# Local attention: dividing probabilities before their transposes instead of scaling the outputs after

## The chip, the cores and the metric

The kernel runs on one core of one Trainium2 chip. The metric is the device time of one execution in microseconds (us). Engines are named as in the profile: PE (TensorE), DVE (VectorE), ACT (ScalarE), POOL (GpSimd), SP (the queue that starts most DMAs).

## What is computed

The reference takes x of 4 batches x 1024 tokens x 256 features. A causal attention with 16 heads comes first; after it come two layers (DEPTH = 2), each with a local attention of 8 heads of 64 features and a feed-forward part. The change lies in the local attention, which in the reference is, cut to what matters:

```python
q = l2norm(q) * qs
k = l2norm(k) * ksc
q, k = rotary_xpos(q, k)
bq = q.reshape(b, h, w, WINDOW, d) * QK_SCALE          # WINDOW = 128
bk, bv = look_around(bk), look_around(bv)              # own window and the one before: 256 keys
sim = jnp.einsum('bhwid,bhwjd->bhwij', bq, bk)
sim = jnp.where(mask, -jnp.finfo(sim.dtype).max, sim)
attn = jax.nn.softmax(sim, axis=-1)
out = jnp.einsum('bhwij,bhwjd->bhwid', attn, bv)
x = x + o @ wo
```

## The kernel before

The program has four stages one after another: `prepare`, `causal_attention` and `project_causal` (up to some 745 us), then `layers`, which holds all that the change touches. `layers` works through eight batches (`it` 0 to 7: two layers of four batches), each as `attention(it)` and then `feed_forward(it)`. A batch has 8 windows of 128 tokens. A window has four units (`PAIRS` = 4) of two heads each, so `attention` runs over 32 units `u`, with w = u // 4 and p = u % 4. Each engine has its own stream, written out by hand as a loop over `u`; its instructions run in that order and wait on counting semaphores for the others.

What one step `u` issues, engine by engine:

- **PE**: `scores` for the units u and u+1 when u is even (L1348, into two PSUM banks), `turn_probs(u-2)` (L1419: four 128x128 transposes of the probabilities), `turn` of the next window's rotated q and k in the steps with p = 0 and 1 (L1328), `project` of the window three ahead in p = 1, 2, 3 (L1302, one third each), and `values` for two units when u is even (L1444). In p = 2 it also has `spread_sums` (L1428), which transposes the widened inverses of the window before. Step 21 and 22 have `project_out` (L1364), 24 and 29 the transposes around the layer norm.
- **ACT**: `copy_probs(u-2)` (L1616), `exponentials(u)` (L1600: two activations with the row sum as second result), the copies of turned q and k (L1592), the high half of x (L1577), `square` (L1563, p = 2), `copy_v` (L1585, p = 3), `widen_sums` (L1625, p = 1) and `copy_output` (L1632, p = 2).
- **DVE**: `mask_scores(u)` (L1865: adds the mask, writes p_sb and the row minimum, for two heads), `unit_vectors(w+2)` in p = 0 (L1842), `times_sin(w+2)` in p = 1 (L1856, four instructions), `low_x` in p = 2 (L1830), `sums(w+3)` in p = 3 (L1836), `invert_sums` (L1917, p = 1) and `scale_output` (L1923, p = 3).
- **POOL**: `rotate`: two multiplications with the cosines (L1758), then, once the four of `times_sin` are done, one addition (L1763); and `norms`: a clamp (L1748) and a power (L1750), which turn the sums of squares into the inverse norms that `unit_vectors` waits for.

The softmax sums are used late before the change: the probabilities go unscaled through transposes and the product with the values, and the output of a window is multiplied afterwards by inverses that have been inverted (DVE), widened (ACT), transposed (PE) and applied (DVE).

## Time and profile before

| what | value |
|---|---|
| median of 3 runs | 2187.49 us (2186.98 to 2192.35) |
| the profiled execution | 2186.37 us, its span 2184.6 us |
| mean granted TensorE clock | 0.968 of full |
| busy: PE, DVE, ACT, POOL | 90%, 66%, 58%, 35% of the span |

The page gives each engine's busy time as a share of the whole span, then the span in 40 slices, the chain of work that ended last, and the costliest groups of instructions. `layers` fills the slices from the fifteenth on. Its attention parts take some 92 us of each batch and its feed-forward parts some 80 us. A line of the timeline is one or several merged instructions of an engine: start, length, engine, line, what is written from what, and in brackets how long the engine sat idle before it and who released it.

### The profile page before, as it was taken

The numbers are of one execution on the slowest core, as the hardware profiler recorded it, in microseconds if no ns is written. First come the engines' busy times: TensorE is split into PE (matmuls) and PEld (weight loads), VectorE is DVE, ScalarE is ACT, GpSimd is POOL, SyncE is SP. The second block draws the span as 40 slices with busy tenths as digits, with TensorE's granted clock in tenths as the row PEclk, the third lists the DMA queues.
The fourth block names the chain that finished last, engine by engine and source line by source line (L and its number), as shares of the span: only waits on it lengthen the run. The fifth ranks groups of instructions, "written<-read, shape, count | busy, mean of one in ns | idle before, by whom it ended". The sixth has DMA issues, their size and how long they took to land.

```text
span 2184.6 us, 36290 instructions
## 1 busy us (share of the span) xinstructions
PE 1969.9 (90%) x12096; PEld 1249.0 (57%) x12096; DVE 1436.6 (66%) x3920; ACT 1264.2 (58%) x3012; POOL 759.6 (35%) x639
## 2 busy tenths in 40 slices
PE   7978999999897459999998999999999999999998
PEld 4522333333224247776676676676677677677666
DVE  7788888888853447557567557656656755755754
ACT  4526666666673227547646746745754764754763
POOL 1033121122322356136236326435515605613620
PEclk9969999999998779999999999999999999999999
DMA  6666533544404610000000000023001000000000
GB/s 181 166 116 139 69 54 50 69 64 87 113 9 134 187 70 13 20 20 2 20 11 11 2 30 11 1 80 111 1 20 39 1 20 20 21 20 20 20 1 30
DMA packets 105271, 112.21 MB, mean 51 GB/s; under 512 B 49708, under 2 KB 84096, under 8 KB 104064
## 3 DMA queue, kind: packets, MB, share of 16 engines
q1 hardware_dynamic: 104512, 100.97, 20.4%
q0 software_dynamic: 576, 8.91, 1.0%
q8 instruction: 100, 1.64, 0.3%
q14 instruction: 83, 0.68, 0.1%
HBM read 67.12 MB, written 42.47 MB: 50 GB/s over the span
## 4 chain that ended last, share of the span: by engine, by line
PE 40%; DVE 11%; ACT 8%; issue 5%; POOL 2%; DMA 0%; SPq 0%; DVEq 0%; POOLq 0%; ACTq 0%
PE qkv_ps L1302 6%; PE s_ps L1406 5%; DVE rot_s L1856 4%; PE s_ps L1348 4%; PE pt_ps L1419 3%; PE o_ps L1487 3%; PE pt_ps L1487 3%; PE qkv_ps L1364 3%; PE o_ps L1444 3%; ACT p_sb L1600 3%; DVE p_sb L1865 3%; PE pt_ps L1406 2%; PE o_ps L1406 2%; PE s_ps L1364 2%; POOL inv_norm L1750 2%
## 5 line engine op out<-in xcount | busy, mean ns | idle before, releaser
L679 ACT ACTIVATE probs<-st_ps 128x512 f32<-128x512 f32 (+3 forms) x768 | 330.0, 494 | 165.6 <-PE st_ps L584 165.1
L1302 PE MATMUL qkv_ps<-w_qkv,x_parts 128*128 128x512 f32 x1152 | 309.1, 412 | 33.6 <-DVE x_parts L1830 24.5
L1600 ACT ACTIVATE p_sb<-p_sb,negmax 128x256 f32<-128x256 f32 (+1 forms) x512 | 249.4, 490 | 65.0 <-DVE negmax L1865 64.8
L569 PE MATMUL s_ps<-k_stack,q_stack 96*128 96x512 bf16 (+3 forms) x768 | 242.6, 347 | 36.6 <-DVE piece_negmax L724 25.6
L724 DVE CUSTOM_DVE_ANT_0 seen<-s_ps,causal 128x128 f32<-128x128 f32 (+3 forms) x512 | 233.8, 484 | 42.1 <-PE s_ps L569 42.0
L1302 PEld LDWEIGHTS qkv_ps<-w_qkv,x_parts 128*128 128x128 f32 x1152 | 212.2, 194 | 81.4 <-issue 39.6
L584 PE MATMUL st_ps<-q_stack,k_stack 98*128 98x512 bf16 (+3 forms) x768 | 241.3, 335 | 12.3 <-ACT probs L679 10.1
L1865 DVE CUSTOM_DVE_ANT_0 p_sb<-s_ps,band 128x256 f32<-128x256 f32 (+1 forms) x512 | 185.5, 401 | 88.7 <-PE s_ps L1348 83.8
L806 POOL TENSOR_SCALAR_AFFINE_SELECT probs<-probs 128x512 f32<-128x512 f32 x128 | 81.6, 637 | 414.5 <-ACT probs L679 414.5
L1758 POOL TENSOR_TENSOR rot_c<-qn,turn_by 128x512 f32<-128x512 f32 x128 | 178.6, 1415 | 129.5 <-PE turn_ps L1328 103.6
L1616 ACT COPY p_t<-pt_ps 128x512 f32<-128x512 f32 (+1 forms) x256 | 143.2, 559 | 125.6 <-PE pt_ps L1419 124.4
L1856 DVE TENSOR_TENSOR rot_s<-qn,turn_by 128x256 f32<-128x256 f32 x256 | 202.9, 851 | 0.3
L727 DVE TENSOR_REDUCE piece_negmax<-s_ps 128x1 f32<-128x512 f32 x256 | 176.0, 687 | 29.4 <-PE s_ps L569 29.1
L1750 POOL TENSOR_TENSOR inv_norm<-sum_sq,neg_half 128x16 f32<-128x16 f32 x64 | 187.6, 2932 | 5.3
L1763 POOL TENSOR_TENSOR rot_c<-rot_c,rot_s 128x1024 f32<-128x1024 f32 x64 | 158.7, 2480 | 60.5 <-DVE rot_s L1856 60.5
L1348 PE MATMUL s_ps<-k_t,q_t 64*128 64x256 f32 (+1 forms) x1152 | 139.5, 364 | 32.0 <-DVE negmax L1865 30.6
L601 PE MATMUL o_ps<-probs,v_all 128*32 128x512 f32 (+3 forms) x1536 | 166.1, 505 | 1.2 <-POOL probs L806 0.7
L1419 PE MATMUL pt_ps<-ident,p_sb 128*128 128x128 f32 x960 | 160.8, 287 | 6.1 <-ACT p_t L1616 6.1
L584 PEld LDWEIGHTS st_ps<-q_stack,k_stack 98*128 98x128 bf16 x768 | 72.1, 98 | 159.4 <-ACT probs L679 124.6
L569 PEld LDWEIGHTS s_ps<-k_stack,q_stack 96*128 96x128 bf16 x768 | 75.7, 99 | 149.5 <-DVE piece_negmax L724 71.4
L1836 DVE TENSOR_REDUCE sum_sq<-squares 128x16 f32<-128x1024 f32 x64 | 77.9, 1217 | 111.4 <-ACT squares L1563 111.4
L1348 PEld LDWEIGHTS s_ps<-k_t,q_t 64*128 64x128 f32 x1152 | 93.0, 187 | 79.8 <-issue 68.4
(145 smaller groups left out, 3452.7 us busy)
## 6 DMA issues: line engine op xcount, KB each, us to landing
qk_scratch<-parts SPq DMA_DIRECT2D x64, 192.0 KB, 2.8
q_stack<-qk_scratch SPq DMA_DIRECT2D x96, 128.0 KB, 6.6
k_stack<-qk_scratch SPq DMA_DIRECT2D x96, 128.0 KB, 7.0
w_ffn<-ffn_weights POOLq DMA_DIRECT2D x4, 2176.0 KB, 11.3
x_in<-xt_scratch SPq DMA_DIRECT2D x16, 512.0 KB, 4.1
ffn_weights<-w_high SPq DMA_DIRECT2D x2, 2176.0 KB, 7.6
ffn_weights<-w_raw SPq DMA_DIRECT2D x2, 2176.0 KB, 13.3
att_scratch<-att SPq DMA_DIRECT2D x32, 128.0 KB, 2.0
```

Source lines behind the costliest of these rows:

```text
L569: pe.matmul(s_ps[i % 3][:, 0:kw], q_stack[0:STK, slot, h, qt * P:(qt + 1) * P], k_stack[0:STK, slot, h, k0:k0 + kw], start=True, stop=True ...
L584: pe.matmul(st_ps[i % 3][:, q0:CH], k_stack[0:STK + SHIFT, slot, h, kt * P:(kt + 1) * P], q_stack[0:STK + SHIFT, slot, h, c * CH + q0:(c + ...
L679: act.activation(probs[:, n % 3, h, q0:CH], st_ps[i % 3][:, q0:CH], ACT.Exp).then_inc(exp_done.sem, 1)
L724: dve.tensor_tensor_reduce(seen[:, i % 3, 0:kw], s_ps[i % 3][:, 0:kw], causal[:, CH - kw:CH], -1.0, BIG, ALU.add, ALU.min, result).then_in ...
L1302: mm = pe.matmul(qkv_ps[:, part * CH:(part + 1) * CH], x_parts[:, w % XR, xp, k, :], w_qkv[:, wp, k, part * INNER:(part + 1) * INNER], sta ...
L1348: mm = pe.matmul(s_ps[side][:, to:to + (t1 - t0) * P], q_t[r, w % 2, p, :], k_t[r, p, t0 % KR * P:(t0 % KR + t1 - t0) * P], start=True, st ...
L1406: mm = pe.matmul(up_pair(c, j)[bank][0:rows, :], w_up(w, k, tile)[:, 0:rows], hn_t[:, h, k, :], start=n == 0, stop=n == len(steps) - 1)
L1419: mm = pe.transpose(pt_ps[:, (h * 2 + kt) * P:(h * 2 + kt + 1) * P], p_sb[:, u % 4, h, kt * P:(kt + 1) * P], ident[:, :])
L1600: act.activation(p_sb[:, u % 4, h, k0:PW], p_sb[:, u % 4, h, k0:PW], ACT.Exp, scale=-1.0, bias=negmax[:, u % 4, h:h + 1], accum_out=total[ ...
L1750: pool.tensor_tensor(inv_norm[:, :], sum_sq[:, 1, :], neg_half[:, 0:2 * H2], ALU.pow)\
L1856: dve.tensor_tensor(dst[:, :, o], src[:, :, i], turn_by[:, w, 2 * j + 1, o].unsqueeze(1) .to_broadcast([P, H2, half]), ALU.mult).then_inc( ...
L1865: dve.tensor_tensor_reduce(p_sb[:, u % 4, h, k0:PW], s_ps[u % 2][:, h * PW + k0:(h + 1) * PW], band[:, k0:PW], 1.0, BIG, ALU.add, ALU.min, ...
```

## The change

Every unit's probabilities are now multiplied by the inverses of their sums in place, by DVE, before PE transposes them. `divide(u)` waits for both exponentials of unit u, takes the reciprocal of two sums per partition, waits for its own result, and multiplies p_sb (128 x 512 elements, 128 x 256 in a batch's first window) with the two inverses, broadcast over 256 columns each. It stands at the head of DVE's step u+1. `turn_probs(u)` waits for it instead of for the exponentials. `invert_sums`, `widen_sums`, `spread_sums` and `scale_output` are gone, with their semaphores and the tile inv_wide; the projection of the outputs waits for ACT's copy.

```diff
-        total = sb("total", [P, 2, PAIRS, 2])
-        inv_total = sb("inv_total", [P, 2, PAIRS, 2])
-        inv_wide = sb("inv_wide", [P, H2, HD2])
+        total = sb("total", [P, 4, 2])
+        inv_total = sb("inv_total", [P, 4, 2])
...
-                if w >= 3 and j == 0:
-                    pe.wait_ge(o_scaled.sem, o_scaled.of(it, w - 3))
...
-                pe.wait_ge(o_scaled.sem, o_scaled.of(it, t1 // P - 1))
+                pe.wait_ge(o_copied.sem, o_copied.of(it, t1 // P - 1))
...
                 def turn_probs(u):
-                    pe.wait_ge(exp_done.sem, exp_done.of(it, 2 * u + 1))
+                    pe.wait_ge(divided.sem, divided.of(it, u))
...
-                def spread_sums(w):
-                    pe.wait_ge(widened.sem, widened.of(it, w))
-                    pe.wait_ge(turn_copied.sem, turn_copied.of(it, 2 * min(w + 2, NT - 1) + 1))
-                    for p in range(PAIRS):
-                        mm = pe.transpose(turn_ps[:, p * P:(p + 1) * P], inv_wide[:, 2 * p:2 * p + 2, :], ident[:, :])
-                    mm.then_inc(spread.sem, 1)
...
-                if u % PAIRS == 0:
-                    act.wait_ge(inv_sum.sem, inv_sum.of(it, w - 2))
...
-                                   accum_out=total[:, w % 2, place(u, h)[0], place(u, h)[1]:place(u, h)[1] + 1]).then_inc(exp_done.sem, 1)
+                                   accum_out=total[:, u % 4, h:h + 1]).then_inc(exp_done.sem, 1)
...
-                def widen_sums(w):
-                    act.wait_ge(inv_sum.sem, inv_sum.of(it, w))
...
-                def invert_sums(w):
-                    dve.wait_ge(exp_done.sem, exp_done.of(it, 2 * (w + 1) * PAIRS - 1))
...
-                def scale_output(w):
-                    dve.wait_ge(spread.sem, spread.of(it, w))
-                    dve.wait_ge(o_copied.sem, o_copied.of(it, w))
...
+                def divide(u):
+                    k0 = 0 if u // PAIRS else WIN
+                    dve.wait_ge(exp_done.sem, exp_done.of(it, 2 * u + 1))
+                    dve.reciprocal(inv_total[:, u % 4], total[:, u % 4]).then_inc(inv_sum.sem, 1)
+                    dve.wait_ge(inv_sum.sem, inv_sum.of(it, u))
+                    probs = p_sb[:, u % 4, :, k0:PW]
+                    dve.tensor_tensor(probs, probs, inv_total[:, u % 4, :].unsqueeze(2).to_broadcast([P, 2, PW - k0]),
+                                      ALU.mult).then_inc(divided.sem, 1)
 
                 for u in range(UNITS + 4):
                     w, p = u // PAIRS, u % PAIRS
+                    if 1 <= u <= UNITS:
+                        divide(u - 1)
                     if p == 2 and w + AHEAD + 1 < NT:
                         low_x(it, w + AHEAD + 1)
```

Where DVE's order changes first: the rows from the q and k of `unit_vectors` to the `sums` of a middle window (L1842 unit_vectors, L1865 mask_scores, L1856 times_sin, L1830 low_x, L1836 sums). Before:

```order
L1842 TENSOR_TENSOR qn<-qkv_ps,inv_norm 128x1024 [waits sin_ready,cos_ready,inv_ready]
L1865 ISA p_sb,negmax<-s_ps,band 128x256 [waits s_ready2,pt_ready]
...
L1917 RECIPROCAL inv_total<-total 128x8 [waits widened,exp_done2]
L1856 TENSOR_TENSOR rot_s<-qn,turn_by 128x8x32 [waits rot_ready,qn_ready]
L1856 TENSOR_TENSOR rot_s<-qn,turn_by 128x8x32 x3
L1830 TENSOR_TENSOR x_parts<-x_in,x_parts 128x256 [waits x_high]
L1865 ISA p_sb,negmax<-s_ps,band 128x256 [waits s_ready2,pt_ready]
...
L1836 TENSOR_REDUCE sum_sq<-squares 128x16 [waits clamped,squared]
```

After (the same steps; L1815 is unit_vectors, L1838 mask_scores, L1829 times_sin, L1803 low_x, L1809 sums, L1889 and L1892 are divide):

```order
L1815 TENSOR_TENSOR qn<-qkv_ps,inv_norm 128x1024 [waits sin_ready,cos_ready,inv_ready]
L1889 RECIPROCAL inv_total<-total 128x2 [waits exp_done2]
L1892 TENSOR_TENSOR p_sb<-p_sb,inv_total 128x512 [waits inv_sum]
...
L1829 TENSOR_TENSOR rot_s<-qn,turn_by 128x8x32 x3
L1889 RECIPROCAL inv_total<-total 128x2 [waits exp_done2]
L1892 TENSOR_TENSOR p_sb<-p_sb,inv_total 128x512 [waits inv_sum]
L1803 TENSOR_TENSOR x_parts<-x_in,x_parts 128x256 [waits x_high]
...
L1892 TENSOR_TENSOR p_sb<-p_sb,inv_total 128x512 [waits inv_sum]
L1809 TENSOR_REDUCE sum_sq<-squares 128x16 [waits clamped,squared]
```

A reciprocal and a multiplication now stand between `unit_vectors` and the next mask, between `times_sin` and `low_x`, and ahead of `sums`; the reciprocal of eight sums is gone.

On PE, step p = 2 of a middle window before:

```order
L1348 MATMUL s_ps<-k_t,q_t 128x256 [waits s_masked,turn_copied]
L1348 MATMUL s_ps<-k_t,q_t 128x256 x3
L1419 MATMUL pt_ps<-ident,p_sb 128x128 [waits pt_copied,exp_done2]
L1419 MATMUL pt_ps<-ident,p_sb 128x128 x3
L1428 MATMUL turn_ps<-ident,inv_wide 128x128 [waits turn_copied,widened]
L1428 MATMUL turn_ps<-ident,inv_wide 128x128 x3
L1302 MATMUL qkv_ps<-w_qkv,x_parts 128x512 [waits qn_ready]
```

and after:

```order
L1343 MATMUL s_ps<-k_t,q_t 128x256 [waits s_masked,turn_copied]
L1343 MATMUL s_ps<-k_t,q_t 128x256 x3
L1414 MATMUL pt_ps<-ident,p_sb 128x128 [waits pt_copied,divided]
L1414 MATMUL pt_ps<-ident,p_sb 128x128 x3
L1299 MATMUL qkv_ps<-w_qkv,x_parts 128x512 [waits qn_ready]
```

The four transposes of inv_wide are gone, and the transposes of the probabilities wait for DVE's `divided` instead of ACT's exponentials.

## Rows read from the trace of the kernel before

**Rows 1.** Page, part 1: busy time, share of the span and instructions of each engine.
```profile
PE 1969.9 (90%) x12096; PEld 1249.0 (57%) x12096; DVE 1436.6 (66%) x3920; ACT 1264.2 (58%) x3012; POOL 759.6 (35%) x639
```

**Rows 2.** Busy time by stretch (from:to in us, length, busy us of each engine, PE clock).
```profile
1174.00:1200.00 26.00, 24.18 (x189) 18.38 (x188) 19.69 (x52) 20.06 (x54) 16.88 (x10) 1.00 0.00 1
```

**Rows 3.** Chain that ended last, in order of time (start, length, engine, tile, line).
```profile
1183.12 0.34 DVE x_parts L1830
...
1184.92 0.57 ACT squares L1563
```

**Rows 4.** Timeline of one window (start, length, engine, line, operation; in brackets idle time before).
```profile
1177.62 1.22 DVE L1842 TENSOR_TENSOR qn<-qkv_ps,inv_norm 128x1024 f32<-128x1024 f32 x1 [0.49 <-POOL inv_norm L1750]
...
1178.76 0.41 DVE L1865 CUSTOM_DVE_ANT_0 p_sb<-s_ps,band 128x256 f32<-128x256 f32 x1
...
1179.56 3.56 DVE L1856 TENSOR_TENSOR rot_s<-qn,turn_by 128x256 f32<-128x256 f32 x4
...
1179.68 2.82 POOL L1758 TENSOR_TENSOR rot_c<-qn,turn_by 128x512 f32<-128x512 f32 x2 [2.09 <-PE turn_ps L1328]
...
1183.04 0.41 DVE L1830 TENSOR_TENSOR x_parts<-x_in,x_parts 128x256 fp32r<-128x256 f32 x1
1183.26 2.44 POOL L1763 TENSOR_TENSOR rot_c<-rot_c,rot_s 128x1024 f32<-128x1024 f32 x1 [0.76 <-DVE rot_s L1856]
1183.38 0.41 DVE L1865 CUSTOM_DVE_ANT_0 p_sb<-s_ps,band 128x256 f32<-128x256 f32 x1
...
1185.86 1.22 DVE L1836 TENSOR_REDUCE sum_sq<-squares 128x16 f32<-128x1024 f32 x1 [1.72 <-ACT squares L1563]
...
1187.00 0.41 DVE L1865 CUSTOM_DVE_ANT_0 p_sb<-s_ps,band 128x256 f32<-128x256 f32 x1
...
1187.91 1.13 PE L1348 MATMUL s_ps<-k_t,q_t 64*128 64x256 f32 x8 [0.51 <-DVE negmax L1865]
...
1188.36 0.19 ACT L1600 ACTIVATION_READ_ACCUMULATOR p_sb<-p_sb,negmax 128x1 f32 x1
...
1190.15 0.51 ACT L1600 ACTIVATE p_sb<-p_sb,negmax 128x256 f32<-128x256 f32 x1
...
1190.58 1.23 DVE L1842 TENSOR_TENSOR qn<-qkv_ps,inv_norm 128x1024 f32<-128x1024 f32 x1 [0.49 <-POOL inv_norm L1750]
```

**Rows 5.** One tile's and one line's instructions: ns least/median/most.
```profile
L1917 DVE RECIPROCAL inv_total<-total x64: 196/198/204, 822.9 to 2114.5; 128x8 f32<-128x8 f32 x64
L1428 PE MATMUL turn_ps<-ident,inv_wide x256: 272/273/328, 825.6 to 2118.6; 128*128 128x128 f32 x128
```

**Rows 6.** Timeline, a feed-forward stretch: DVE work beside POOL work.
```profile
1121.69 1.42 DVE L1856 TENSOR_TENSOR rot_s<-qn,turn_by 128x256 f32<-128x256 f32 x4
...
1123.04 0.68 DVE L1964 TENSOR_TENSOR hidden<-gate,hidden 128x512 fp32r<-128x512 f32 x1
...
1123.27 2.72 POOL L1763 TENSOR_TENSOR rot_c<-rot_c,rot_s 128x1024 f32<-128x1024 f32 x1 [1.44 <-DVE rot_s L1856]
...
1124.48 1.79 DVE L1830 TENSOR_TENSOR x_parts<-x_in,x_parts 128x256 fp32r<-128x256 f32 x1
...
1133.83 2.93 POOL L1750 TENSOR_TENSOR inv_norm<-sum_sq,neg_half 128x16 f32<-128x16 f32 x1
...
1135.06 0.41 DVE L1830 TENSOR_TENSOR x_parts<-x_in,x_parts 128x256 fp32r<-128x256 f32 x1
```

**Rows 7.** Timeline, DVE in the sixth window.
```profile
1222.89 0.43 DVE L1865 CUSTOM_DVE_ANT_0 p_sb<-s_ps,band 128x256 f32<-128x256 f32 x1 [1.23 <-PE s_ps L1348]
```

**Rows 8.** Timeline, PE from the seventh window to the last unit.
```profile
1228.60 1.13 PE L1348 MATMUL s_ps<-k_t,q_t 64*128 64x256 f32 x8
...
1248.69 0.66 PE L1419 MATMUL pt_ps<-ident,p_sb 128*128 128x128 f32 x4
```

**Rows 9.** Timeline and busy time where the granted clock fell in the second batch.
```profile
989.95 1.44 PE L1348 MATMUL s_ps<-k_t,q_t 64*128 64x256 f32 x8 [2.03 <-DVE negmax L1865]
...
990.50:994.00 3.50, 3.50 (x21) 2.20 (x18) 1.90 (x5) 2.30 (x8) 2.35 (x1) 0.52 0.03 7
```

More of the change, by code:

```diff
@@ L1144, in layers @@
         exp_done = count("exp_done2", 2 * UNITS)
-        inv_sum = count("inv_sum", NT, 2)
-        widened = count("widened", NT)
-        spread = count("spread", NT)
-        o_scaled = count("o_scaled", NT)
+        inv_sum = count("inv_sum", UNITS)
+        divided = count("divided", UNITS)
         pt_ready = count("pt_ready", UNITS, 4)
@@ L1462, in attention @@
                         final_tiles(it - 1, 1, 1, turn_ps)
-                    if u >= PAIRS + 2 and (u - 2) % PAIRS == 0:
-                        spread_sums((u - 2) // PAIRS - 1)
                     if p >= 1 and w + AHEAD < NT:
@@ L1618, in copy_probs @@
                        .then_inc(pt_copied.sem, 1)
-                def widen_sums(w):
-                    act.wait_ge(inv_sum.sem, inv_sum.of(it, w))
-                    if w:
-                        act.wait_ge(spread.sem, spread.of(it, w - 1))
-                    act.copy(inv_wide[:, :, :], inv_total[:, w % 2].rearrange("p a s -> p (a s)").unsqueeze(2)
-                             .to_broadcast([P, H2, HD2])).then_inc(widened.sem, 1)
                 def copy_output(w):
@@ L1648, in attention @@
                         copy_v(it, w + AHEAD)
-                    if u >= PAIRS + 1 and (u - 1) % PAIRS == 0:
-                        widen_sums((u - 1) // PAIRS - 1)
                     if u >= PAIRS + 2 and (u - 2) % PAIRS == 0:
@@ L1814, in _ @@
         def _(dve):
-            for c in (qn_ready, sin_ready, s_masked, inv_sum, mid_ready, hn_t_split, hidden_ready, hidden_split, out_ready):
+            for c in (qn_ready, sin_ready, s_masked, mid_ready, hn_t_split, hidden_ready, hidden_split, out_ready):
                 dve.sem_inc(c.sem, c.credit)
@@ L1912, in attention @@
             def attention(it):
-                def invert_sums(w):
-                    dve.wait_ge(exp_done.sem, exp_done.of(it, 2 * (w + 1) * PAIRS - 1))
-                    if w >= 2:
-                        dve.wait_ge(widened.sem, widened.of(it, w - 2))
-                    dve.reciprocal(inv_total[:, w % 2], total[:, w % 2]).then_inc(inv_sum.sem, 1)
-                def scale_output(w):
-                    dve.wait_ge(spread.sem, spread.of(it, w))
-                    dve.wait_ge(o_copied.sem, o_copied.of(it, w))
-                    window = o_t[:, :, w % WPC * P:(w % WPC + 1) * P]
-                    dve.tensor_tensor(window, turn_ps[:, :].rearrange("p (h t) -> p h t", h=PAIRS), window, ALU.mult)\
-                       .then_inc(o_scaled.sem, 1)
+                def divide(u):
[6 more added lines that the diff above has]
+                                      ALU.mult).then_inc(divided.sem, 1)
                 for u in range(UNITS + 4):
                     w, p = u // PAIRS, u % PAIRS
+                    if 1 <= u <= UNITS:
+                        divide(u - 1)
                     if p == 2 and w + AHEAD + 1 < NT:
@@ L1933, in attention @@
                         mask_scores(it, u)
-                    if u >= PAIRS + 1 and (u - 1) % PAIRS == 0:
-                        invert_sums((u - 1) // PAIRS - 1)
-                    if u >= PAIRS + 3 and (u - 3) % PAIRS == 0:
-                        scale_output((u - 3) // PAIRS - 1)
                     if it > B and u in (1, 3):
```

## The prediction

> **What bounds the kernel now.** I read the busy shares first: PE 90%, DVE 66% [rows 1]. That looks like a kernel bound by PE, and the change takes work from PE. So I looked at a stretch of two middle windows: in 26 us PE is busy 24.18, DVE 19.69, ACT 20.06 [rows 2]. PE is nearly full there, but the chain that ended last does not stay on it. In each window it runs through DVE's `times_sin`, `low_x`, `mask_scores`, ACT's exponentials and squares, DVE's `sums` and POOL's power (two of its links are shown) [rows 3]. The timeline of one window gives the loop in numbers [rows 4]. I call the start of `unit_vectors` Q (1177.62). `mask_scores` of p = 1 starts at Q+1.14, `times_sin` at Q+1.94 and issues its last at about Q+5.1, `low_x` starts at Q+5.42, the mask of p = 2 at Q+5.76, and `sums` at Q+8.24, when the exponentials and the squares behind that mask are done (2.48 after it). The next `unit_vectors` follows 4.72 after `sums` (1185.86 to 1190.58), because POOL must clamp and raise to a power first. 5.76 + 2.48 + 4.72 = 12.96, the window's period. PE has no term in this loop. So what counts is how late the mask of p = 2 comes after Q, and whether `unit_vectors` stays tied to `sums`.
>
> `times_sin` holds the key. Its four instructions take 1.42 us when POOL leaves them alone (the first line of that stretch) [rows 6], and 3.56 here, with POOL's two cosine multiplications (2.82 us) beside them [rows 4]. In the feed-forward part a `low_x` that takes 0.41 us elsewhere took 1.79: it started 1.21 us into a POOL addition and ended 0.28 us after it [rows 6]. So a DVE instruction with two SBUF inputs stands still until the POOL multiplication or addition has ended. The masks and `unit_vectors`, which read PSUM, do not: the mask of p = 2 takes 0.41 inside the addition [rows 4].
>
> **What the change adds and removes.** A `divide` is a reciprocal (0.20 us for eight sums [rows 5]; I take the same for two), the wait for its own result (no row has one; between nothing and 0.2, I take 0.14, nearest to the 0.145 between `times_sin`'s end and POOL's start [rows 4]) and a multiplication of 128x512 with two SBUF inputs, for which the nearest row is 0.68 [rows 6], some 0.61 from issue to issue. That is 0.95 us, between 0.80 and 1.05, four per window; 0.8 us of old DVE work goes.
>
> In the loop, from Q:
> - The divide of p = 0 stands behind `unit_vectors`: Q+1.14 to Q+2.09. The mask of p = 1 then ends at Q+2.78. POOL's cosine multiplications still start at Q+2.06, so `times_sin` begins inside the first of them; it loses less than it started late, since in both kernels it waits for both of POOL's. It catches up to a last start of Q+5.42, 0.34 later than now.
> - The divide of p = 1 stands right behind it, where `low_x` stood. Its reciprocal starts at Q+5.76 and its multiplication would at Q+6.1. POOL's addition starts 0.145 after the last sine product, at Q+5.98, and takes 2.44. The multiplication has two SBUF inputs, so it waits to Q+8.41 and ends its issue at Q+9.0. `low_x` follows, and the mask of p = 2 starts at Q+9.34 instead of Q+5.76: **3.6 us later**.
> - The divide of p = 2 waits for exponentials that end 1.55 after their mask (1187.00 to 1188.55 [rows 4]), and 1.55 + 0.95 = 2.50, as long as the squares take (2.48). It costs nothing, but if ACT's squares were earlier it would cost all of its 0.95.
> - The divide of p = 3 ends 1.14 + 1.55 + 0.95 = 3.64 after the start of `sums`; the mask behind it ends at 4.33, before 4.72. POOL's power hides it, with 0.4 us to spare.
>
> Period: 9.34 + 2.48 + 4.72 = 16.5 against 12.96. Five windows of a batch have `sums` and `times_sin` (the first with narrower units, the fifth without `low_x`; I take 3.6 for each): 18.0 us. In the sixth the mask of p = 2 waits for PE anyway, at Q+6.7 (1222.89, idle 1.23 until the scores [rows 7]), and two products with w_out keep PE full after it; the late mask is hidden there, and I take 0, with up to 1.5 if that cover is thin.
>
> The windows seven and eight have no rotation. There a pair of units now is one round: scores to the first exponential 2.24 (1187.91 to 1190.15), both exponentials 1.10, a divide 0.95, the second mask to the next scores 0.91 (1187.00 to 1187.91) [rows 4]: 5.2. Three rounds are 15.6. From the last scores to the last transposes it is 2.24 + 1.10 + 0.95, then mask to exponential 0.45, exponentials 1.10, divide 0.95 and 0.1: 6.9. Together 22.5, against 20.09 now (1228.60 to 1248.69 [rows 8]); less 0.44 for the last transposes of inv_wide: plus 2.0, between 0.5 and 3.5.
>
> On PE four transposes per window go. They are 0.27 us each and overlap, at most 0.60 for four by their pipelined starts and ends [rows 5]; in five windows they lie outside the loop and bring nothing. ACT loses a wide copy per window, also outside it. No DMA moves.
>
> PE will stand idle in the longer windows, in one piece of some 2.7 us ahead of the scores of p = 0. Now it idles 2.03 us at one such place in a batch's first window, and in the second batch the granted clock fell to 0.52 of full (so to the 1.2 GHz level) for the 3.5 us behind it; the scores took 1.44 instead of 1.13 [rows 9, 4]. Half of 40 windows with such a fall, some 1 us of PE's work later each, half of it reaching the loop, is 10 us; between 0 and 40.
>
> **Sum:** 8 batches x (18.0 + 0 + 2.0) = 160, and 10 for the clock: 170 us on the profiled execution's 2186.4 is 2356.4. The median of the runs shown lies 1.1 higher, so I say **2357 us**, 7.8% slower. (Within 0.3%, 6.6 us, is what a measurement of this kernel can't tell from no change.)
>
> The Trainium skill, page "SBUF — State Buffer", section "Who interferes with whom", says that a DVE instruction with two SBUF inputs contends with a GpSimd one that reads SBUF, and that whoever issues first keeps the shared port for its whole instruction. For the cosine products and the addition the trace agrees (1.79 against 0.41 us). By the letter of that rule POOL's power would block the divide of p = 3 too; that is rival 3.
>
> **Rivals.**
> 1. The multiplication goes first. It misses POOL's addition by only 0.12 us (Q+6.1 against Q+5.98). If it wins, `low_x` is the one that waits (that happened in [rows 6]), and in four windows nothing changes; only the fifth, without `low_x`, gains 2.3. 8 x 2.3 = 18 less: 2339. For it: the small margin. Against it: the wait for its own result. Chance 0.17.
> 2. The multiplication isn't held and neither is `low_x`, so only DVE's own work counts: 0.34 + 0.95 = 1.3 per window. 8 x (5 x 1.3 + 2.0) = 68: 2255. Against it: the 1.79 us. For it: no row shows a multiplication right behind `times_sin`, and a hold depends on who is first. Chance 0.08.
> 3. POOL's power holds it as well. The power starts 1.75 after `sums` and ends at 4.68; the multiplication of p = 3 would start at 3.0, wait to 4.68, and `unit_vectors` would come at 6.0 instead of 4.72: 1.3 in 40 windows, 50 us more, 2407. Against it: a `low_x` of 0.41 us lies wholly inside a power of 2.93 [rows 6]. Chance 0.07.
> 4. The clock falls in nearly all windows and the loop gets all of it: 30 us more, 2387. Chance 0.10.
> 5. It gets faster: DVE's gaps take the divides and PE sets the period. DVE is busy 9.85 of 12.96 us in a window [rows 2], so 3.1 are idle, and the change adds 4 x 0.95 - 0.8 = 3.0; by busy time it just fits. Then 64 times at most 0.60 us of PE goes: 38 us, 2149. The point from which it decides is the mask of p = 2: it has to start by Q+5.8. Against it: the idle time is not where the divides stand; 1.72 of it lies behind that mask, waiting for squares that the mask itself releases [rows 4]. Chance 0.03.
>
> **How the numbers follow.** My forecast has 0.55. The range takes it with its bounds (tail, sixth window, clock: about 2330 to 2385), rival 1 and rival 4, and stretches toward 2 and 3: 2305 to 2405. Slower by over 0.3%: all but rival 5, 0.96; within 0.3%: 0.01, if gains and losses meet; faster: 0.03.
>
> **What would show it.** Right: the period from one `unit_vectors` to the next is about 16.5 us in windows two to five; the multiplication behind `times_sin` lasts some 2.9 us and ends just after POOL's addition, while the others take 0.7; `sums` still starts 2.5 after the mask of p = 2, and `unit_vectors` 4.7 after `sums`; PE idles some 2.7 us ahead of the scores. Rival 1 shows as a long `low_x`, rival 2 as periods near 14.3, rival 3 as a long multiplication within the power, rival 4 as a granted clock well under 1 in the attention slices. The prediction is wrong if the mask of p = 2 starts before Q+8.

## The result, and the profile after

The changed kernel takes **2343.71 us** (median of 4 runs, 2338.77 to 2345.07) against 2188.62 for the kernel before (2186.98 to 2192.35): a ratio of 1.0702 with the interval 1.068 to 1.0724 (1.071 from the two medians). Its profiled execution took 2344.4 us, with a span of 2342.7 against 2184.6, so 158 us are to be found in the trace.

The busy times of the changed kernel, as [rows 1] has it for the kernel before:

```profile
PE 1993.5 (85%) x11840; PEld 1265.5 (54%) x11840; DVE 1656.7 (71%) x4304; ACT 1231.5 (53%) x2948; POOL 782.1 (33%) x639
```

PE has 256 matmuls fewer and is busy 24 us longer. That is the first hint of the clock, whose mean over the span fell from 0.968 to 0.937. DVE is busy 220 us longer. Its new instructions account for 209 (224 multiplications of 0.69, 32 narrower ones of 0.42, 256 reciprocals of 0.16), and those removed take 57 off (64 scalings of 0.69 and 64 reciprocals of 0.20). Some 70 us are left over, and one line holds them: the 64 `low_x` take 105.8 us together instead of 35.2. They stood still, and the profile counts that as busy.

The periods from one `unit_vectors` to the next, as means over the eight batches, show where the 158 us lie (worked out from the starts of that line; "first" is the first window that has `sums` and `times_sin` in it, and the last number runs from a batch's last `unit_vectors` to the next batch's first, leaving out the step from one layer to the next):

```
          first  second  third  fourth  fifth    rest
before    12.17  12.77   12.95  12.96   12.65    73.6
after     15.18  16.93   17.22  16.96   14.75    75.5 to 76.7
more       3.0    4.2     4.3    4.0     2.1     2 and more
```

That is 17.6 in five windows and 2.0 behind them: 8 x 19.6 = 157 us.

The timeline of one window of the changed kernel (start, duration, engine, line; in brackets the engine's idle time before it), the counterpart of [rows 4]. Q is 1208.16:

```profile
1208.16 1.22 DVE L1815 TENSOR_TENSOR qn<-qkv_ps,inv_norm 128x1024 f32<-128x1024 f32 x1 [0.36 <-POOL inv_norm L1723]
...
1210.78 3.14 DVE L1829 TENSOR_TENSOR rot_s<-qn,turn_by 128x256 f32<-128x256 f32 x4
1213.84 0.15 DVE L1889 RECIPROCAL inv_total<-total 128x2 f32<-128x2 f32 x1
1214.03 0.69 DVE L1892 TENSOR_TENSOR p_sb<-p_sb,inv_total 128x512 f32<-128x512 f32 x1
1214.06 2.89 POOL L1736 TENSOR_TENSOR rot_c<-rot_c,rot_s 128x1024 f32<-128x1024 f32 x1 [1.10 <-DVE rot_s L1829]
1214.64 2.60 DVE L1803 TENSOR_TENSOR x_parts<-x_in,x_parts 128x256 fp32r<-128x256 f32 x1
1217.16 0.41 DVE L1838 CUSTOM_DVE_ANT_0 p_sb<-s_ps,band 128x256 f32<-128x256 f32 x1
...
1218.94 0.69 DVE L1892 TENSOR_TENSOR p_sb<-p_sb,inv_total 128x512 f32<-128x512 f32 x1
1219.65 1.22 DVE L1809 TENSOR_REDUCE sum_sq<-squares 128x16 f32<-128x1024 f32 x1
...
1221.39 2.93 POOL L1723 TENSOR_TENSOR inv_norm<-sum_sq,neg_half 128x16 f32<-128x16 f32 x1
...
1221.70 2.08 PE L1343 MATMUL s_ps<-k_t,q_t 64*128 64x256 f32 x8 [4.62 <-DVE negmax L1838]
...
1222.57 0.69 DVE L1892 TENSOR_TENSOR p_sb<-p_sb,inv_total 128x512 f32<-128x512 f32 x1
...
1223.70 1.12 PE L1414 MATMUL pt_ps<-ident,p_sb 128*128 128x128 f32 x4
1224.04 0.42 DVE L1838 CUSTOM_DVE_ANT_0 p_sb<-s_ps,band 128x256 f32<-128x256 f32 x1 [0.78 <-PE s_ps L1343]
...
1224.74 1.22 DVE L1815 TENSOR_TENSOR qn<-qkv_ps,inv_norm 128x1024 f32<-128x1024 f32 x1
```

The multiplication in step p = 1 starts at 1214.03, 0.03 us before POOL's addition, and keeps its normal 0.69. The addition takes 2.89 where it takes 2.44 in [rows 4]. `low_x`, 0.41 when free, then takes 2.60 and ends 0.29 behind the addition. The mask of p = 2 starts at Q+9.00. `sums` comes 2.49 behind it, as before. The mask comes 3.24 us later than before (Q+5.76), in three parts: `times_sin` ends 0.26 later behind the first divide, the divide of p = 1 itself takes 0.80 (1213.84 to 1214.64), and `low_x` takes 2.19 longer. So DVE's plain work is a third of it, and the standing still two thirds. The multiplication of p = 3 lasts 0.69 and lies wholly inside POOL's power (1221.39 to 1224.32).

The scores took 2.08 us where they took 1.13 [rows 4], after PE had been idle for 4.62. Four stretches of the changed kernel (from:to, length, busy time and count of PE, PEld, DVE, ACT, POOL, then the granted clock, and the share and GB/s of the DMAs):

```profile
1208.20:1224.70 16.50, 11.88 (x70) 8.61 (x70) 13.94 (x30) 8.41 (x25) 8.78 (x5) 0.81 0.00 0
1217.00:1221.00 4.00, 0.08 (x1) 0.00 (x0) 3.14 (x9) 2.96 (x7) 0.00 (x0) 0.81 0.00 0
1221.00:1223.00 2.00, 1.30 (x6) 1.22 (x8) 1.15 (x6) 1.56 (x5) 1.86 (x2) 0.50 0.00 0
1223.00:1228.00 5.00, 5.00 (x37) 3.85 (x36) 3.68 (x13) 2.41 (x7) 1.32 (x1) 0.67 0.01 3
```

In the first row PE is busy 11.88 of 16.5; in [rows 2] it was 24.18 of 26. In the second PE does next to nothing, and the clock falls inside it (0.81 is the mean of the 4 us). In the third the granted clock is 0.50, the 1.2 GHz level, and it stays there through part of the fourth, while PE is busy all the time. Over the five windows of all eight batches the clock is at that level for 156 us in 32 stretches; before, it was for 10 us in 3. The same sum is given for the runs below.

How that reaches the loop can be read off the chain that ended last (start, us, what), the counterpart of [rows 3]:

```profile
1210.87 3.06 DVE rot_s L1829 x4
...
1214.64 2.60 DVE x_parts L1803
1217.24 0.33 DVE p_sb L1838
...
1221.70 2.08 PE s_ps L1343 x8
1223.77 1.06 PE pt_ps L1414 x4
...
1225.75 0.69 ACT p_sb L1583 x3
1226.46 0.18 DVE inv_total L1889
```

On its way into the next window the chain no longer goes through POOL's power. It goes through the slow scores. They end late, so the mask behind them waits 0.78 us for PE and holds up `unit_vectors`. That starts 0.42 after the power's end (1224.32), and 5.09 after `sums` instead of 4.72. The slow transposes delay ACT's copy and exponentials, and the next window's first reciprocal starts at Q+1.72 instead of Q+1.14. Together that is 0.37 + 0.58, some 0.95 us.

### The profile page after: what moved, and what is told of

Same layout as the page of the kernel before. It is cut to its first block, busy times and chain, and to the rows that moved or that the text cites. A ratio compares the mean times of both kernels' runs of the same rounds, so it can differ in the third digit from the quotient of the medians.

```text
span 2342.7 us, 35801 instructions
## 1 busy us (share of the span) xinstructions
PE 1993.5 (85%) x11840; PEld 1265.5 (54%) x11840; DVE 1656.7 (71%) x4304; ACT 1231.5 (53%) x2948; POOL 782.1 (33%) x639
## 4 chain that ended last, share of the span: by engine, by line
PE 33%; DVE 19%; ACT 7%; issue 7%; POOL 2%; DMA 0%; DVEq 0%; SPq 0%; POOLq 0%; ACTq 0%
DVE rot_s L1829 6%; PE qkv_ps L1299 5%; PE s_ps L1401 4%; ACT p_sb L1583 4%; DVE p_sb L1838 4%; PE s_ps L1343 4%; DVE x_parts L1803 4%; PE o_ps L1472 3%; PE pt_ps L1472 3%; PE qkv_ps L1359 3%; PE pt_ps L1414 2%; PE pt_ps L1401 2%; PE o_ps L1401 2%; PE s_ps L1359 2%; POOL inv_norm L1723 2%
## 5 line engine op out<-in xcount | busy, mean ns | idle before, releaser
L1343 PE MATMUL s_ps<-k_t,q_t 64*128 64x256 f32 (+1 forms) x1152 | 160.1, 405 | 165.3 <-DVE negmax L1838 165.3
L1343 PEld LDWEIGHTS s_ps<-k_t,q_t 64*128 64x128 f32 x1152 | 106.3, 209 | 214.7 <-issue 210.4
L1838 DVE CUSTOM_DVE_ANT_0 p_sb<-s_ps,band 128x256 f32<-128x256 f32 (+1 forms) x512 | 186.3, 401 | 22.1 <-PE s_ps L1343 21.6
L1736 POOL TENSOR_TENSOR rot_c<-rot_c,rot_s 128x1024 f32<-128x1024 f32 x64 | 178.8, 2793 | 60.5 <-DVE rot_s L1829 60.3
L1829 DVE TENSOR_TENSOR rot_s<-qn,turn_by 128x256 f32<-128x256 f32 x256 | 197.4, 830 | 0.1
L1414 PE MATMUL pt_ps<-ident,p_sb 128*128 128x128 f32 x960 | 174.9, 306 | 15.7 <-ACT p_t L1599 8.8
L1892 DVE TENSOR_TENSOR p_sb<-p_sb,inv_total 128x512 f32<-128x512 f32 (+1 forms) x256 | 175.5, 685 | 8.7
```

What stands on the lines that cost most here:

```text
L1343: mm = pe.matmul(s_ps[side][:, to:to + (t1 - t0) * P], q_t[r, w % 2, p, :], k_t[r, p, t0 % KR * P:(t0 % KR + t1 - t0) * P], start=True, st ...
L1414: mm = pe.transpose(pt_ps[:, (h * 2 + kt) * P:(h * 2 + kt + 1) * P], p_sb[:, u % 4, h, kt * P:(kt + 1) * P], ident[:, :])
L1829: dve.tensor_tensor(dst[:, :, o], src[:, :, i], turn_by[:, w, 2 * j + 1, o].unsqueeze(1) .to_broadcast([P, H2, half]), ALU.mult).then_inc( ...
L1838: dve.tensor_tensor_reduce(p_sb[:, u % 4, h, k0:PW], s_ps[u % 2][:, h * PW + k0:(h + 1) * PW], band[:, k0:PW], 1.0, BIG, ALU.add, ALU.min, ...
```

## The experiments

Two theories stand at the start. **The hold**: the loss comes from an instruction of DVE with two SBUF inputs that stands still until a POOL addition or multiplication is over (I call it held), in front of the mask of p = 2. **PE's clock**: most of what the windows lost beyond that comes from the lower clock that an idle PE is granted. The rivals are DVE's plain work, and the sheer number of waits.

### What stands in front of the mask

**low_x behind the mask of p = 2:**

```diff
                     if 1 <= u <= UNITS:
                         divide(u - 1)
-                    if p == 2 and w + AHEAD + 1 < NT:
-                        low_x(it, w + AHEAD + 1)
...
                     if EARLY <= u < UNITS:
                         mask_scores(it, u)
+                    if p == 2 and w + AHEAD + 1 < NT:
+                        low_x(it, w + AHEAD + 1)
```

> One instruction moved on DVE: low_x of step p = 2 stands behind the mask instead of between the divide and the mask. Theory A (the hold: low_x waits for POOL's addition and the mask of p = 2 stands behind it): that mask starts some 2.5 us earlier, at about Q+7.5 instead of Q+10; low_x stays as long as it is, since it still waits for the addition, and holds the divide of p = 2 and sums a little, so a window gets 1.4 to 1.5 us shorter in the first four windows of a batch: 4 x 1.5 x 8 = 48 us less, about 2296 us. Theory B (DVE simply has more work per window): the same instructions, no change, 2344 us within 10.

Measured: 2274.08 us, ratio 1.0399 [1.038, 1.0418]. The timeline of this kernel:

```profile
1216.05 0.69 DVE L1892 TENSOR_TENSOR p_sb<-p_sb,inv_total 128x512 f32<-128x512 f32 x1
1216.09 2.89 POOL L1736 TENSOR_TENSOR rot_c<-rot_c,rot_s 128x1024 f32<-128x1024 f32 x1 [1.10 <-DVE rot_s L1829]
1216.66 0.42 DVE L1838 CUSTOM_DVE_ANT_0 p_sb<-s_ps,band 128x256 f32<-128x256 f32 x1
...
1217.35 1.92 DVE L1803 TENSOR_TENSOR x_parts<-x_in,x_parts 128x256 fp32r<-128x256 f32 x1
```

The mask of p = 2 starts inside the addition and is not held. `low_x` still is (1.92), but in time in which DVE had nothing else to do. One moved instruction gives 70 us back, nearly half of the loss. I had expected 48. The windows tell how much of it is the hold: where the clock did not fall, a middle window takes 14.5 us instead of the 16.2 that it takes in the changed kernel's order (see under "The clock"), and the first went from 15.2 to 13.5. Four windows of 1.7 in 8 batches are 54 us. That leaves 16 for the clock, whose lower level fell from 156 to 73 us. That the same instructions in another order take 70 us less rules out DVE's plain work as the cause of that part.

**Each divide behind the mask of its step:** (in this kernel low_x stands where the changed kernel has it)

```diff
-                    if 1 <= u <= UNITS:
-                        divide(u - 1)
                     if p == 2 and w + AHEAD + 1 < NT:
                         low_x(it, w + AHEAD + 1)
...
                     if EARLY <= u < UNITS:
                         mask_scores(it, u)
+                    if 1 <= u <= UNITS:
+                        divide(u - 1)
```

> The divides stand behind the mask of their step instead of at its head; nothing is added or taken away. Theory A: the mask of p = 2 starts at about Q+6.0, low_x slips in before POOL's addition (0.41 us), the multiplication of p = 1 is held by the addition for about 2 us instead, in time that DVE spent waiting for the squares; no mask waits for an exponential any more, in the windows without rotation either. Period of a middle window about 14.0 instead of 17.1; per batch some 14 us less, 2344 - 115 = about 2229 us. Theory B (the work itself): the divides cost their 0.95 us wherever they stand, 32 x 0.95 less the 0.81 of old work per window is 24 us per batch, more than the whole loss; the time stays within 20 us of 2344.

Measured: 2251.55 us, ratio 1.0303 [1.0282, 1.0324]. Its timeline:

```profile
1197.03 2.98 POOL L1731 TENSOR_TENSOR rot_c<-qn,turn_by 128x512 f32<-128x512 f32 x2 [2.17 <-PE turn_ps L1323]
...
1197.25 1.63 DVE L1892 TENSOR_TENSOR p_sb<-p_sb,inv_total 128x512 f32<-128x512 f32 x1
...
1201.22 0.41 DVE L1803 TENSOR_TENSOR x_parts<-x_in,x_parts 128x256 fp32r<-128x256 f32 x1
1201.44 2.40 POOL L1736 TENSOR_TENSOR rot_c<-rot_c,rot_s 128x1024 f32<-128x1024 f32 x1 [1.43 <-DVE rot_s L1829]
1201.55 0.41 DVE L1838 CUSTOM_DVE_ANT_0 p_sb<-s_ps,band 128x256 f32<-128x256 f32 x1
...
1202.24 0.15 DVE L1889 RECIPROCAL inv_total<-total 128x2 f32<-128x2 f32 x1
1202.43 1.97 DVE L1892 TENSOR_TENSOR p_sb<-p_sb,inv_total 128x512 f32<-128x512 f32 x1
```

Now two multiplications per window are held, and `low_x` gets through ahead of the addition. The reciprocal inside the addition, with one SBUF input, keeps its 0.15. Middle windows in which the clock did not fall take 14.1 us, as I had worked out (14.0). The sum was 22 us short: eight of the later windows take 15.5 to 16.1, and each of them has a stretch at the lower clock in its second half (55 us in all).

### Which part of the divide costs

**The changed kernel without its multiplications:** the reciprocals and their waits stay; the outputs are not divided by the sums.

```diff
-                    dve.reciprocal(inv_total[:, u % 4], total[:, u % 4]).then_inc(inv_sum.sem, 1)
-                    dve.wait_ge(inv_sum.sem, inv_sum.of(it, u))
-                    probs = p_sb[:, u % 4, :, k0:PW]
-                    dve.tensor_tensor(probs, probs, inv_total[:, u % 4, :].unsqueeze(2).to_broadcast([P, 2, PW - k0]),
-                                      ALU.mult).then_inc(divided.sem, 1)
+                    dve.reciprocal(inv_total[:, u % 4], total[:, u % 4]).then_inc(divided.sem, 1)
```

> The changed kernel without the multiplications (the reciprocals stay, and the transposes wait for them; probabilities and outputs stay unscaled). Theory A: with 0.8 us less between times_sin and low_x, low_x starts ahead of POOL's addition or just with it; where it does, the mask of p = 2 starts at about Q+6.1 instead of 9 to 10 and a middle window takes about 13.4 us. The reciprocals still wait for the exponentials ahead of each mask, so the windows without rotation stay about 1 us longer than before. 2186.8 + 8 x (5 x 0.45 + 1) = about 2213 us, or 2290 if low_x is still held. Theory B (the loss is DVE's own added work): 32 multiplications of 0.61 us gone per batch, 156 us: 2188 us.

Measured: 2178.66 us, ratio 0.9963 [0.9948, 0.9977]. Its timeline:

```profile
1181.62 0.15 DVE L1889 RECIPROCAL inv_total<-total 128x2 f32<-128x2 f32 x1
1181.70 0.40 DVE L1803 TENSOR_TENSOR x_parts<-x_in,x_parts 128x256 fp32r<-128x256 f32 x1
1181.85 2.49 POOL L1736 TENSOR_TENSOR rot_c<-rot_c,rot_s 128x1024 f32<-128x1024 f32 x1 [0.76 <-DVE rot_s L1829]
1182.02 0.41 DVE L1838 CUSTOM_DVE_ANT_0 p_sb<-s_ps,band 128x256 f32<-128x256 f32 x1
```

`low_x` starts 0.15 us ahead of the addition and is free; the period is 13.0. The fair comparison is the kernel before without its scaling, which also leaves the outputs undivided: 2178.13 us (see below). The two agree, so all of the loss comes with the multiplications, and the reciprocals and the waits for ACT cost nothing that can be seen. Whether the multiplications cost by their own time or by the hold this run can't tell; the two moves above do. Both numbers I had written down were too high, the one for the hold by 34 us: I had left `low_x` held behind the reciprocal, though a reciprocal alone is short enough for it to get in first.

**The multiplication as two with a scalar per partition:** one input of 128x256 from SBUF, and the inverse as the scalar.

```diff
-                    dve.tensor_tensor(probs, probs, inv_total[:, u % 4, :].unsqueeze(2).to_broadcast([P, 2, PW - k0]),
-                                      ALU.mult).then_inc(divided.sem, 1)
+                    for h in range(2):
+                        ins = dve.tensor_scalar(p_sb[:, u % 4, h, k0:PW], p_sb[:, u % 4, h, k0:PW],
+                                                inv_total[:, u % 4, h:h + 1], None, ALU.mult)
+                    ins.then_inc(divided.sem, 1)
```

> The changed kernel, but each divide multiplies with two instructions of 128 x 256 that take the inverse as a scalar per partition: one SBUF tensor goes in instead of two. Theory A (only instructions with two SBUF inputs and POOL exclude each other): POOL's addition behind times_sin no longer waits for the multiplication ahead of it and takes 2.44 us instead of 2.89, so it ends some 0.4 us earlier, and low_x, still held by it, too; a held multiplication (up to 1.57 us) is not to be seen any more. 4 windows x 0.4 x 8 = 14 us less, plus or minus the difference between one multiplication and two (at most 0.1 us each): 2325 to 2340 us. Theory E (every DVE instruction on SBUF takes part): the addition stays at 2.9 us, and the time at 2344 or above.

Measured: 2342.1 us, ratio 1.0703 [1.0674, 1.0733], no change against the changed kernel. Its timeline:

```profile
1212.27 2.80 DVE L1893 TENSOR_SCALAR p_sb<-p_sb,inv_total 128x256 f32<-128x256 f32 x2
1212.30 2.35 POOL L1736 TENSOR_TENSOR rot_c<-rot_c,rot_s 128x1024 f32<-128x1024 f32 x1 [1.10 <-DVE rot_s L1829]
1214.99 0.41 DVE L1803 TENSOR_TENSOR x_parts<-x_in,x_parts 128x256 fp32r<-128x256 f32 x1
```

A free pair, behind `unit_vectors` in the same window, takes 0.62, the pair at the addition 2.80, until after the addition's end (1214.65); then `low_x` is free. The hold does not ask for two tensors from SBUF: a multiplication with one, and a scalar operand, is held too. My expectation had it free, and that part of the theory falls. Its rival (the addition stays at 2.9) isn't what happened either: the pair's first half starts 0.03 us ahead of the addition, as the multiplication of the changed kernel did, yet here it is the one that waits (2.54), and the addition takes 2.35.

Not every instruction with one SBUF input is held, as the reciprocal of 0.15 shows in the run with the divides behind the masks. What sets this form apart in the rows is its speed: free, it takes 0.28 us for 128x128 and 0.35 for 128x256, so 0.07 for 128 columns more, where the form with two tensors takes 0.42 and 0.69 for 256 and 512, 0.13 for 128 more. Whether that is why it is held was not tested.

The unchanged time hides two shifts. The middle windows' mean fell from 17.0 to 16.4: in four batches the fourth window takes 14.8, since `low_x` starts just ahead of the addition there and takes 0.41. And the fifth window, where the pair is now held, grew from 14.75 to 16.2.

**Both: the scalar form, and behind the mask** (the two edits above together).

> The divides behind the masks (as in e2_div_after) and the multiplications with scalars per partition. In e2_div_after the multiplication of p = 0 lasts 1.63 us inside POOL's cosine products and that of p = 1 lasts 1.96 us inside POOL's addition. Theory A: both drop to two pieces of about 0.4 us in the very same place, sums starts 0.3 us earlier, when the squares are ready (2.48 behind the mask), and windows of 14.1 us go to about 13.8: 5 x 0.3 x 8 = 12 us less than 2251.6, about 2240 us. Theory E: both stay above 1.5 us, no change.

Measured: 2224.18 us, ratio 1.0175 [1.0157, 1.0194], the best of the versions that divide the probabilities. Its timeline:

```profile
1190.57 2.57 POOL L1731 TENSOR_TENSOR rot_c<-qn,turn_by 128x512 f32<-128x512 f32 x2 [2.17 <-PE turn_ps L1323]
1190.74 2.55 DVE L1893 TENSOR_SCALAR p_sb<-p_sb,inv_total 128x256 f32<-128x256 f32 x2
1193.21 1.42 DVE L1829 TENSOR_TENSOR rot_s<-qn,turn_by 128x256 f32<-128x256 f32 x4
```

The pair is held to just after the end of the second cosine multiplication (1193.14), and the four sines then take 1.42, their free time. Both forms of the multiplication and the sines stand still beside POOL's 2.6 us, and here the pair does so in the place of the sines. Only 17 us are left at the lower clock, the windows take 13.5 to 13.8 us on average, and their lengths hardly differ. I had expected 2240 for a reason that did not come true: both pairs are held. The time came out lower all the same. The windows in which the clock did not fall are 0.3 us shorter than with the form of two tensors (13.8 against 14.1), and there is less of the lower clock (17 us instead of 55).

**A second reciprocal ahead of the multiplication of p = 1** (in the changed kernel), to let POOL's addition go first:

```diff
                     dve.wait_ge(exp_done.sem, exp_done.of(it, 2 * u + 1))
+                    if u % PAIRS == 1:
+                        dve.reciprocal(spare[:, :], total[:, u % 4])
                     dve.reciprocal(inv_total[:, u % 4], total[:, u % 4]).then_inc(inv_sum.sem, 1)
```

> The changed kernel with a second reciprocal (to a spare tile) in the divide of p = 1 alone, so that its multiplication comes 0.08 us later, behind the start of POOL's addition instead of 0.03 us ahead of it. Theory A (who starts first holds the other): the multiplication now lasts some 2.9 us and low_x 0.41; the addition takes 2.44 instead of 2.89. A middle window gets 0.3 to 0.4 us shorter, since the addition no longer waits; the fifth window, which has no low_x, gets 1.5 to 2.0 us longer (14.8 to 16.6). 8 x (4 x 0.35 - 1.8) = 3 us less to more: 2338 to 2350 us, with these two shifts of the windows. If 0.08 us more work only adds up, both kinds of window get 0.08 longer.

Measured: 2355.3 us, ratio 1.0767 [1.0745, 1.0789]. Its timeline (lines are one to three higher):

```profile
1233.43 0.14 DVE L1892 RECIPROCAL inv_total<-total 128x2 f32<-128x2 f32 x1
1233.57 2.38 POOL L1737 TENSOR_TENSOR rot_c<-rot_c,rot_s 128x1024 f32<-128x1024 f32 x1 [0.42 <-DVE rot_s L1830]
1233.60 2.90 DVE L1895 TENSOR_TENSOR p_sb<-p_sb,inv_total 128x512 f32<-128x512 f32 x1
1236.42 0.41 DVE L1804 TENSOR_TENSOR x_parts<-x_in,x_parts 128x256 fp32r<-128x256 f32 x1
...
1241.30 1.13 PE L1344 MATMUL s_ps<-k_t,q_t 64*128 64x256 f32 x8 [2.70 <-DVE negmax L1839]
```

This is the collision of my prediction, brought about on purpose: POOL is first by 0.03 us, the multiplication takes 2.90 and `low_x` 0.41. PE then idles 2.70 us ahead of the scores, and in this window they take 1.13. The fifth window, which has no `low_x`, grew from 14.75 to 15.6 on average, and that mean mixes two kinds: in four batches POOL is first there and the window takes 16.0 to 17.3, in the other four the multiplication meets a cosine multiplication instead, and the window takes 14.85. So for this multiplication the order is decided by hundredths of a us, and it costs where nothing else was going to wait. The time is 5 us above the end of what I had expected. My sum had nothing for the stretch behind the five windows, which grew by 0.9 us a batch, 7 in all: the feed-forward part takes 0.3 more in each batch, and what is left of the sixth window takes 13.1 us instead of 12.0 in four batches (in two in the changed kernel). Why was not tested.

### The clock

**Work for PE in the gap:** 16 transposes of the identity, whose results nobody reads, behind the last third of the projection in five windows (1 <= w <= 5).

```diff
                         project(it, w + AHEAD, p - 1)
+                    if 3 <= u < UNITS - 8 and p == 3 and w >= 1:
+                        if it > B:
+                            pe.wait_ge(fin_added.sem, fin_added.of(it - 1 - B, 3))
+                        pe.wait_ge(turn_copied.sem, turn_copied.of(it, 2 * w + 3))
+                        for i in range(16):
+                            pe.transpose(turn_ps[:, i % 4 * P:(i % 4 + 1) * P], ident[:, :], ident[:, :])
```

> The changed kernel with 16 transposes of the identity (results not used) behind the last third of project in windows two to six, about 1.8 us of PE work in the place where PE now idles ahead of the scores of p = 0. Theory D (the idle PE is granted a lower clock behind the gap, and the slower scores and transposes cost the loop 0.6 us a window): the scores of p = 0 take 1.13 us again, mean granted clock goes up from 0.937, windows of 17.1 go to 16.5, 3 x 0.6 x 8 = 15 us less, about 2329 us. If the clock has no part in the loss: no gain, and at most a few us more.

Measured: 2340.92 us, ratio 1.0696 [1.0675, 1.0717]. The stretch of 5 us in which the changed kernel had a granted clock of 0.67, in this one:

```profile
1223.00:1228.00 5.00, 4.26 (x41) 3.41 (x42) 3.70 (x13) 4.19 (x12) 3.11 (x2) 1.00 0.00 0
```

In the five middle windows in which the clock did not fall at all, a window takes 16.16 to 16.18 us instead of 17.2; the fifth window then takes 13.97 instead of 14.75 (three of them). The middle windows' mean went from 17.0 to 16.5, 12 us in all, while the lower level fell from 156 to 89 us. The rest of the batch gives most of that back (from between 75.5 and 76.7 to 77.0): between its last `unit_vectors` and the seventh window's scores it takes 13.7 us in every batch, where the changed kernel takes 12.0 in six of eight. The last filling stands in that very place. So the time alone would have told nothing, and it missed the 2329 that I expected; the windows tell that the clock is worth about 0.9 us of each middle window.

**The same in three windows only** (1 <= w <= 3), to spare the end of the batch:

> As e4_fill, but the 16 transposes of the identity stand in windows two, three and four only. In e4_fill the middle windows went from 17.0 to 16.5 on average while the end of each batch grew by 1.3 us (76.98 against 75.5 us), since window six has no idle PE to fill. Theory D (the clock): the same three windows stay short and the end keeps its 75.5: about 10 us less than e4_fill, 2325 to 2333 us. If the end grows all the same, the filling isn't what costs there, and the time stays at 2341.

Measured: 2337.97 us, ratio 1.0689 [1.0665, 1.0714], 5 us over the end of what was expected. The end of the batch stayed as in the changed kernel (12.0 again in seven of eight batches), so the filling was what had made it longer. Some middle windows came to 16.2, others took up to 17.6, with 93 us at the lower level. Filling a gap does not secure the clock, and no run has it at the upper level throughout.

### What the removed work was worth

**The kernel before without widening, spreading and scaling** (its outputs are not divided by the sums): the three calls go, with the waits on what they produced, of which one is shown; the reciprocals stay.

```diff
-                    pe.wait_ge(o_scaled.sem, o_scaled.of(it, w - 3))
...
-                        spread_sums((u - 2) // PAIRS - 1)
...
-                        widen_sums((u - 1) // PAIRS - 1)
...
-                        scale_output((u - 3) // PAIRS - 1)
```

> The kernel before, without widen_sums, spread_sums and scale_output (the outputs of the local attention stay unscaled; the reciprocals stay). It shows what the removed part was worth by itself. Theory A (a window is bound by the chain over DVE, ACT and POOL, in which PE has no term): only the end of each batch's attention gets shorter, by 0.4 to 1 us, 3 to 8 us in all: 2180 to 2185 us. Theory C (PE sets the period): 64 groups of four transposes at 0.44 to 0.60 us, 28 to 38 us less: 2150 to 2160 us.

Measured: 2178.13 us, ratio 0.9959 [0.9944, 0.9974]. The windows' periods are unchanged, and the rest of the batch went from 73.6 to 72.4. So the work that the change takes away, but for one reciprocal a window, was worth 9 us, at the end of the batch; in the windows PE's transposes and DVE's scaling were hidden. The rival in which PE is the bound (2150 to 2160) is out.

### A version that beats both

**The kernel before, with low_x at the end of step p = 3:**

```diff
-                    if p == 2 and w + AHEAD + 1 < NT:
-                        low_x(it, w + AHEAD + 1)
...
                         mask_scores(it, u)
+                    if p == 3 and w + AHEAD + 1 < NT:
+                        low_x(it, w + AHEAD + 1)
```

> The kernel before with low_x moved from step p = 2, where it stands between times_sin and the mask, to the end of step p = 3, behind sums and the mask. Theory A (the mask of p = 2 is a term of the loop, and low_x in front of it costs its 0.34 us even where nothing holds it): windows of 12.96 go to 12.62 in the four windows that have a low_x, 4 x 0.34 x 8 = 11 us less: 2176 us. If PE sets the period of a window (24.2 of 26 us busy), nothing changes.

Measured: 2177.01 us (8 runs), ratio 0.9954 [0.9939, 0.9968]. Its timeline:

```profile
1179.77 0.41 DVE L1865 CUSTOM_DVE_ANT_0 p_sb<-s_ps,band 128x256 f32<-128x256 f32 x1
...
1184.08 0.43 DVE L1830 TENSOR_TENSOR x_parts<-x_in,x_parts 128x256 fp32r<-128x256 f32 x1
```

The mask of p = 2 starts at Q+5.42 instead of Q+5.76, `low_x` stands in DVE's idle time beside POOL's power, unheld, and a window takes 12.62 instead of 12.96. By the loop of the prediction that is 0.34 in each of four windows, 8 x 4 x 0.34 = 11 us, and 10 were measured. That is 0.5% less than the kernel before takes, and 7% less than the changed one.

## Why the prediction was right, and where not

The time is right: 13 us under the forecast and inside the range. The loop behind it is right too: the mask of p = 2 comes 3.2 us later, `sums` 2.49 behind it, and at the upper clock PE has no term. But one step of the account failed, several sizes were off, and that the total still fits is in part luck. Rival 1's 2339 is nearer to the measured 2343.7 than my 2357, and I had given it 0.17.

- **The order at the collision (failed).** "Its reciprocal starts at Q+5.76 and its multiplication would at Q+6.1", after the addition at Q+5.98. It was the other way round: reciprocal Q+5.68, multiplication Q+5.87, addition Q+5.90. I had given the wait for its own result 0.14 us and the reciprocal 0.20; together they took 0.19. So rival 1 was what happened: `low_x` was held. In four windows it makes no difference which of the two waits, as the rival said. The fifth, without `low_x`, lost 1.3 by it instead of 3.6 (13.97 without a fall of the clock, against 12.65), just the 2.3 less that the rival had. Where the second reciprocal brings the predicted order about, that window takes 16.0 in three batches, some 2 us more.
- **The middle windows.** I had 16.5 with the clock counted apart; without falls of the clock they take 16.2, with them 16.9 to 17.2 on average. The mask of p = 2 came at Q+9.00, not Q+9.34. That `sums` follows the mask by 2.5 was right. The 4.72 from there to `unit_vectors` holds only at the upper clock; with the slow scores it is 5.1.
- **The clock (mis-sized).** I had 10 us, from PE idling 2.7 us ahead of the scores. It idled 4.62 in the window shown and 3.1 to 4.6 in 32 places: the multiplication of p = 1 wasn't held, so PE did its transposes and the projection behind them early, and all of the wait lies in one piece. In the predicted order, in the run with a second reciprocal, it was 2.70. The lower level comes in 32 stretches in the 40 windows instead of the 20 I took. From the windows that kept the clock in the filled run, it costs (17.04 - 16.16) x 3 x 8 = 21 us in the middle windows and (14.75 - 13.97) x 8 = 6 in the fifth, 27 in all. That is an estimate, and it is near rival 4's 30 us (chance 0.10).
- **The first window:** +3.0 against 3.6; its units are narrower, and I didn't look into it further.
- **The end of the batch:** +2.0, as predicted, but the parts are not the predicted ones. From the seventh window's first scores to the last transposes' end it takes 3.1 us more (23.8 against 20.75), not 2.0; the sixth window's remainder takes 0.4 less and the feed-forward part 0.7 less, which I had at nothing. The sixth window's late mask cost nothing, as I had taken.
- **The sum again:** 3.0 + 3 x 3.3 + 1.3 + 2.0 = 16.2 per batch and some 130 in all, and 27 for the clock: 157 of 158. I had 160 and 10. The two errors, 30 too much for the windows and 17 too little for the clock, had opposite signs, and that is the luck in it.
- **POOL's power (rival 3):** refuted by the multiplication of 0.69 inside it. The letter of the Trainium skill's rule (page "SBUF — State Buffer", section "Who interferes with whom") would have held it; the measurement decides. Rival 2's hold-free windows came in no run that multiplies; even the best order, at 2224 us, has two held pairs per window.
- **PE as the bound (rival 5):** refuted by the run without scaling, 9 us where 38 were on offer.

What stays open: what the clock costs in full, since no run kept it; why the scalar form is held, and gives way to an addition that starts behind it; and why the end of the batch grew with the second reciprocal. A second buffer for the rotated q and k, which would let POOL's work move away from DVE's, was not tried.

## What to carry to other kernels

When an instruction is put into a busy engine's order, look at what stands behind it and who waits for that, not at its own time: here four divides in a window, 0.80 us of DVE's time each, cost a middle window 3.3 us and the clock's 0.9 on top, since one instruction of DVE was pushed into a POOL operation that it can't run beside, with a mask behind it. Put such an instruction behind the one that others wait for; one move gave back 70 of the 158 us, and the same reading of the old kernel gave 10 us. Work taken off an engine that looks 90% busy is worth what its wait in the loop was, here nearly nothing.

## What the runs showed that I had not expected

All multiplications of the changed kernel, grouped by their line (durations in ns, least, median and most). Their median is the free time: the one that waits is mostly `low_x`. The most, 1.57 us, shows that some of them are held too:

```profile
L1892 DVE TENSOR_TENSOR p_sb<-p_sb,inv_total x256: 424/691/1570, 810.1 to 2273.5; 128x512 f32<-128x512 f32 x112, 128x256 f32<-128x256 f32 x16
```

- An instruction that is held shows as a longer one, not as idle time. POOL's side is stretched in the same way when it comes second: the addition takes 2.89 us behind a multiplication of two tensors that was first by 0.03, and 2.38 when it is first itself.
- A multiplication with one SBUF tensor and a scalar per partition is held like one with two tensors (2.80 us for a pair that takes 0.62 free), even where it starts 0.03 us ahead of the addition, and it does not stretch it (2.35). A reciprocal of 128x2 inside the addition is not held (0.15).
- POOL's power of 128x16 holds nothing, over 2.93 us; its addition of 128x1024 and its multiplications of 128x512 do.
- DVE's wait for its own reciprocal costs 0.04 us beyond the reciprocal's 0.15.
- PE idle for 3.1 to 4.6 us ahead of the scores in most windows goes with a granted clock of 0.50 in 32 stretches, and the scores behind the gap of 4.62 take 2.08 us instead of 1.13.
